# Graph attention layer on one core: eight unread products between two turnings, magnitudes of heads 8 to 15 a head earlier, their store made contiguous

## The chip, the cores and the metric

The kernel runs on one core of one Trainium2 chip. The metric is the device time of one launch in microseconds. A core has a matrix engine (TensorE, PE in the profile, with its weight loads shown apart as PEld), VectorE (DVE), ScalarE (ACT), GpSimd (POOL), and SyncE (SP), which here only issues DMAs. Each engine works through its own instructions in order; semaphores are the only thing that ties them together.

## The reference, cut to what matters

```python
# x: (2048, 512), adj: (2048, 2048) of zeros and ones; N = 2048, H = 16 heads, DH = 32, ALPHA = 0.2
seq = (x @ W_seq).reshape(N, H, DH)
score1 = jnp.einsum('nhd,d->hn', seq, a1)
score2 = jnp.einsum('nhd,d->hn', seq, a2)
scores = leaky_relu(score1[:, :, None] + score2[:, None, :], ALPHA)
scores = scores + (1.0 - adj)[None, :, :] * MASK_VAL
attn = softmax(scores, axis=-1)
hidden = einsum('hij,jhd->ihd', attn, seq).reshape(N, D_IN)
hidden = elu(hidden @ W_out + b_out)
return layernorm(x + hidden)
```

## The kernel before

A score is a sum of a row term and a column term, so the leaky exponential splits into two products of a row factor and a column factor, one for positive and one for negative sums. What is left of the softmax for one head is a mask (is the sum positive, and is there an edge) times a matrix of values. All masks are one byte per element and are read as fp8. The values are split into a high and a low half in f16, in `Vp`.

**Stages.** Up to about 85 us: load x, W and the adjacency matrix; PE turns x (L387) and two of the four parts of W (`turn_w`, L424), multiplies the turned W by the attention vectors (L431), and projects x (L400, then L416 for heads 8 to 15); ACT casts 16 adjacency tiles to bytes (L592), DVE patches them (L782), and SP's DMAs turn them (L316). `warm(n)` (L379) issues n products of 256 columns whose result nobody reads. From there to 450 us: the heads. Behind that: the output product (L568), elu and layer norm.

**A head.** For head h and each of 16 tiles jt, the sign of the score is made by ACT (L614) or by DVE (L811, six tiles of a head in heads 1 to 12: 2, 3, 6, 7, 12, 13); DVE then joins tiles in pairs with the edges (L816), which counts `t_ready` up by two. PE runs 16 products for each tile (L475) as soon as its pair is ready. Behind tile 7 and behind tile 15 it runs two blocks of products against the whole adjacency matrix (`adj_products`, L489, 32 products a block). The first such block of a group of four heads waits until all four heads' values are split: block 16, in the middle of head 4, waits for the values of head 7. The ring `tring` holds 16 tiles, one head's worth, so makers of the signs can be at most a head ahead of PE. When PE is through with a head, ACT copies the low sums (L652), DVE adds the high ones (`join`, L879, behind tile 4 of the next head), and PE may begin the next head.

**Values.** Beside head h (1 to 12) DVE and ACT make the values of head h + 3: DVE's product (L860, behind tile 1), ACT's high halves (L631), DVE's low halves (`split_low`, L866, behind tile 9). Values are scaled by a power of two taken from the largest magnitude of the head. For heads 8 to 15 this is found in three steps. DVE takes the largest of four parts (`largest`, L792) at the places in the table `MAX_AT`, and joins them in head 3 behind tile 14 (L979, `mx2_ready`). SP stores the 128 x 8 maxima to DRAM (L349, `maxima`) and loads them back spread over all partitions (L351, 128 x 1024), before it loads the row of head 5 (L352). SP gets there only once all pairs of head 3 are joined. DVE takes the largest of each head (L982, in head 4 behind tile 7), makes the powers, and goes on. L982 stands ahead of the pair of tiles 8 and 9 and of the low halves of head 7.

The order on every engine is written out by hand; no scheduler changes it. `DVE_TILES`, `MAX_AT`, `HIGH_AT` and `LOW_AT` say behind which tile something stands.

Of the kernel before, what the change touches and what calls it, by code (L numbers as in the profile page):

```python
# [10 lines left out]
ALU = mybir.AluOpType  # L11
ACT = mybir.ActivationFunctionType
AX = mybir.AxisListType

P = 128
# [49 lines left out]

FIRST_AT, ROUND_AT = {9: (0, 1), 15: (2,)}, {15: (0, 1)}

MAX_AT = {(2, 9): 0, (2, 13): 1, (3, 5): 2, (3, 9): 3}

SUMS_AT = (None,) + (4,) * (H - 1)  # L70
VALUES_AT, HIGH_AT, LOW_AT = 1, 6, 9
# [22 lines left out]
def gat_kernel(nc, x, adj, W_seq, a1, a2, W_out, b_out, out):  # L94
    with ExitStack() as ctx:
# [3 lines left out]
        def sem(name):  # L99
            return ctx.enter_context(nc.semaphore(name))  # L100
# [27 lines left out]
        peaks = flat[:, 10 * HV:10 * HV + 2 * P * HALF].bitcast(F32)  # L128
# [3 lines left out]
        ones, mx, mx2, mcol = misc[:, 0:P], misc[:, 128:128 + MC], misc[:, 160:160 + HALF], misc[:, 192:193]  # L132
# [22 lines left out]
        def pair(k):  # L155
# [19 lines left out]
        scratch2 = nc.dram_tensor("maxima", [1, P * HALF], F32, kind="Internal")  # L175
# [17 lines left out]
        mx2_part, mx2_ready, mx2_stored, peaks_loaded, peak_made = (  # L193
            sem(s) for s in ("mx2_part", "mx2_ready", "mx2_stored", "peaks_loaded", "peak_made"))
# [78 lines left out]
        def row(h):  # L273

            return abc[:, (h + 1) % 2, :] if h > 0 else row0
# [18 lines left out]
        def _(sp):  # L294
# [46 lines left out]
            for h in range(1, H):  # L341
                if h == 2:
                    sp.wait_ge(seq2_made, NT)
                if h >= 2:
                    sp.wait_ge(t_ready, NT * (h - 1))
                if h == 5:

                    sp.wait_ge(mx2_ready, 1)
                    sp.dma_start(scratch2.rearrange("o (h p) -> (o p) h", p=P), mx2, allow_slow_non_contiguous=True).then_inc(mx2_stored, 16)  # L349
                    sp.wait_ge(mx2_stored, 16)  # L350
                    sp.dma_start(peaks, scratch2[0:1, :].partition_broadcast(P)).then_inc(peaks_loaded, 16)  # L351
                sp.dma_start(row(h), scratch[h:h + 1, :].partition_broadcast(P)).then_inc(abc_loaded[h % 2], 16)  # L352
# [22 lines left out]
        def _(pe):  # L375
            def warm(n, into=bank[2]):

                for _ in range(n):
                    pe.matmul(into[:, 0:2 * P], ones16[:, 0:P], ones16, start=True, stop=True)  # L379
# [39 lines left out]
            def turn_w(n):  # L419

                k = BY_PE[n]
                pe.wait_ge(w_loaded[k], 16)
                for j in range(KT):
                    mm = pe.transpose(bank[6 + n][:, j * P:(j + 1) * P], Wx[:, k, j // 2, j % 2 * P:(j % 2 + 1) * P], idf)  # L424
                mm.then_inc(w_turned, 1)
# [26 lines left out]
            pe.wait_ge(ident, 1)  # L452
            turn_x(0)
            turn_w(0)
            turn_w(1)
            warm(4)
            pe.wait_ge(block_ready, 1)
# [92 lines left out]
            for i in range(NT + 1):  # L550
# [7 lines left out]
                if i >= 1:  # L558
                    q = (i - 1) % 2
# [197 lines left out]
        def _(dve):  # L757
# [208 lines left out]
            for h in range(1, H):  # L966
                row_loaded(dve, h)
                for jt in range(NT):
                    if jt + 1 in DVE_TILES[h]:
                        compare(h, jt + 1)  # L970
                    if jt % 2 == 1:
                        made(h, jt // 2)
                        join_adj(jt // 2, WHOLE).then_inc(t_ready, 2)
                    if (h, jt) in MAX_AT:
                        dve.wait_ge(seq2_copied, NT)
                        largest(MAX_AT[h, jt], mxd[:, MAX_AT[h, jt], :], slice(HALF, H)).then_inc(mx2_part, 1)
                    if h == 3 and jt == 14:
                        dve.wait_ge(mx2_part, 4)
                        dve.tensor_reduce(mx2, mxd.rearrange("p c k -> p k c"), AX.X, ALU.max).then_inc(mx2_ready, 1)  # L979
                    if h == 4 and jt == 7:  # L980
                        dve.wait_ge(peaks_loaded, 16)
                        dve.tensor_reduce(mx2, peaks.rearrange("p (h q) -> p h q", q=P), AX.X, ALU.max).then_inc(peak_made, 1)  # L982
                        dve.wait_ge(peak_made, 1)
                        powers(slice(HALF, H), mx2, 1)
                    if h == 4 and jt == 10:
# [186 lines left out]
```

## Time and profile before

| | us |
|---|---|
| median of 3 runs | 518.84 (518.45 to 519.27) |
| the profiled execution | 522.9 |
| its span | 521.2 |
| PE busy | 503.4 (97%) |
| DVE busy | 459.6 (88%) |
| ACT busy | 433.7 (83%) |
| L475, mask products, 4096 | 241.8 |
| L489, adjacency products, 2048 | 127.7 |

The span is the time between the first and the last instruction that the profiler saw; 1.7 us of the profiled execution lie around it. Its time is 4.1 us above the median of the three runs without a profiler. A busy share is an average over the whole span: what matters in a stretch is which engine the others wait for there, and that is read from the chain of waits and from the timelines.

### The profile page before, as it was taken

The numbers are of one execution on the slowest core, as the hardware profiler recorded it, in microseconds if no ns is written. First come the engines' busy times: TensorE is split into PE (matmuls) and PEld (weight loads), VectorE is DVE, ScalarE is ACT, GpSimd is POOL, SyncE is SP. The second block draws the span as 40 slices with busy tenths as digits, with TensorE's granted clock in tenths as the row PEclk, the third lists the DMA queues.
The fourth block names the chain that finished last, engine by engine and source line by source line (L and its number), as shares of the span: only waits on it lengthen the run. The fifth ranks groups of instructions, "written<-read, shape, count | busy, mean of one in ns | idle before, by whom it ended". The sixth has DMA issues, their size and how long they took to land.

```text
span 521.2 us, 15251 instructions
## 1 busy us (share of the span) xinstructions
PE 503.4 (97%) x6744; PEld 456.7 (88%) x6744; DVE 459.6 (88%) x577; ACT 433.7 (83%) x462; POOL 34.8 (7%) x64
## 2 busy tenths in 40 slices
PE   7999999999999989999999999999999999899993
PEld 5788889999999889999999999999999999644542
DVE  3266899998999898999999999999998879988886
ACT  2477899798999887999999999999995989356664
POOL 3000000000000010000000000000000000035444
PEclk9899999999999989999999999999999999999998
DMA  7999995202020411201021120202202040015343
GB/s 258 395 302 344 333 332 142 86 3 82 3 83 2 115 38 55 83 3 82 3 83 31 54 83 3 83 1 83 79 7 82 3 143 3 1 62 159 122 141 122
DMA packets 31617, 53.28 MB, mean 102 GB/s; under 512 B 19392, under 2 KB 20672, under 8 KB 27584
## 3 DMA queue, kind: packets, MB, share of 16 engines
q1 hardware_dynamic: 31000, 51.79, 30.5%
q8 instruction: 53, 0.87, 0.7%
q10 hardware_dynamic: 552, 0.52, 0.3%
q14 instruction: 12, 0.10, 0.1%
HBM read 43.78 MB, written 4.33 MB: 92 GB/s over the span
## 4 chain that ended last, share of the span: by engine, by line
PE 80%; DVE 9%; DMA 4%; ACT 3%; issue 2%; POOL 0%; ACTq 0%; POOLq 0%; DVEq 0%
PE sums L475 35%; PE bank L489 19%; PE sums L568 10%; PE sums L400 6%; PE sums L416 4%; DVE tring L816 3%; ACT tring L614 2%; DVE tring L811 2%; DMA maxima<-Vp 2%; PE sums L387 1%; PE bank L416 1%; PE bank L556 1%; DMA Vp<-in_L_gnn_W_seq_dram 1%; DMA Vp<-maxima 1%; DVE Vp L792 1%
## 5 line engine op out<-in xcount | busy, mean ns | idle before, releaser
L614 ACT ACTIVATE tring<-abc,ab 128x2048 int8<-128x2048 f32 x150 | 292.2, 2019 | 2.0 <-PE sums L475 2.0
L475 PE MATMUL sums<-Vp,tring 128*128 128x132 f16 x4096 | 241.8, 221 | 3.5 <-issue 2.4
L475 PEld LDWEIGHTS sums<-Vp,tring 128*128 128x128 fp8e4 x4096 | 236.9, 98 | 5.5 <-issue 3.5
L816 DVE TENSOR_TENSOR tring<-adj,tring 128x1024 uint32<-128x1024 uint32 (+1 forms) x134 | 155.9, 1174 | 13.6 <-ACT tring L614 9.1
L489 PE MATMUL bank<-Vp,adj 128*128 128x132 f16 x2048 | 127.7, 222 | 2.1 <-DVE Vp L866 2.1
L489 PEld LDWEIGHTS bank<-Vp,adj 128*128 128x128 fp8e4 x2048 | 123.8, 97 | 2.3 <-DVE Vp L866 2.3
L811 DVE TENSOR_SCALAR tring<-abc,ab 128x2048 int8<-128x2048 f32 x90 | 115.5, 1283 | 0.0
L568 PE MATMUL sums<-abc,Vp 128*128 128x512 f32 (+1 forms) x136 | 57.5, 568 | 0.1
L568 PEld LDWEIGHTS sums<-abc,Vp 128*128 128x128 f32 x136 | 24.7, 190 | 22.7 <-issue 22.0
L652 ACT ACTIVATE low<-sums 128x33 f32<-128x33 f32 (+3 forms) x66 | 20.1, 393 | 24.1 <-PE sums L475 24.0
L592 ACT ACTIVATE tring<-Vp 128x2048 int8<-128x2048 f32 x16 | 30.6, 1911 | 1.2 <-DMA Vp<-in_adj_dram 1.2
L752 ACT ACTIVATE Vp<-Vp 128x512 f32<-128x512 f32 x15 | 12.2, 813 | 16.4 <-POOL Vp L1145 16.4
L879 DVE TENSOR_TENSOR cab<-low,sums 128x66 f32<-128x66 f32 (+3 forms) x33 | 21.2, 682 | 1.9 <-ACT low L652 1.9
L637 ACT ACTIVATE acc<-bank 128x132 f32<-128x132 f32 x64 | 18.6, 290 | 4.1 <-PE bank L489 3.3
L866 DVE SCALAR_TENSOR_TENSOR Vp<-Vp,xp 128x528 f16<-128x528 f16 x32 | 21.2, 706 | 0.1
L860 DVE TENSOR_TENSOR xp<-acc,Es 128x1056 f32<-128x1056 f32 x16 | 20.0, 1252 | 0.1
L631 ACT ACTIVATE Vp<-xp 128x528 f16<-128x528 f32 x32 | 19.6, 677 | 0.6 <-DVE xp L860 0.6
L400 PE MATMUL sums<-Vp,acc 128*128 128x288 f32 x64 | 19.0, 441 | 0.0
L787 DVE COPY ab<-sums 128x32 f32<-128x32 f32 x16 | 3.0, 189 | 17.0 <-PE sums L400 17.0
L743 ACT ACTIVATE Vp<-Vp 128x512 f32<-128x512 f32 (+1 forms) x17 | 10.2, 602 | 8.3 <-DVE Vp L1041 8.2
L1041 DVE TENSOR_TENSOR Vp<-sums,Vp 128x512 f32<-128x512 f32 (+1 forms) x17 | 11.2, 658 | 6.6 <-PE sums L568 6.6
L811 DVE TENSOR_SCALAR tring<-cab,ab 128x2048 int8<-128x2048 f32 (+2 forms) x16 | 14.7, 951 | 2.3 <-ACT cab L601 2.2
(116 smaller groups left out, 369.7 us busy)
## 6 DMA issues: line engine op xcount, KB each, us to landing
Vp<-in_adj_dram SPq DMA_DIRECT2D x16, 1024.0 KB, 8.1
abc<-a_rows SPq DMA_DIRECT2D x15, 1024.0 KB, 4.8
abc<-in_x_dram SPq DMA_DIRECT2D x16, 256.0 KB, 7.4
Vp<-in_x_dram SPq DMA_DIRECT2D x16, 256.0 KB, 2.9
out_dram<-Vp SPq DMA_DIRECT2D x16, 256.0 KB, 2.0
abc<-in_L_gnn_W_out_dram SPq DMA_DIRECT2D x1, 1024.0 KB, 5.3
Vp<-in_L_gnn_W_seq_dram ACTq DMA_DIRECT2D x2, 256.0 KB, 5.4
Vp<-in_L_gnn_W_seq_dram SPq DMA_DIRECT2D x2, 256.0 KB, 6.1
```

Source lines behind the costliest of these rows:

```text
L400: mm = pe.matmul(first_bank(t), xT_part(t, k), Wx[:, k, 0, :], start=(k == BY_VECTOR[0]), stop=(k == BY_VECTOR[1]))
L416: mm = pe.matmul(second_bank(t), xT_part(t, k), Wx[:, k, 1, 0:half], start=(k == 0), stop=(k == KT - 1))
L475: mm = pe.matmul(bank[b][:, c * 2 * VW:(c + 1) * 2 * VW], slot(jt)[:, it * P:(it + 1) * P].bitcast(F8), Vp[:, h, jt, :, :], start=(jt == 0 ...
L489: mm = pe.matmul(bank[6 + s % 2][:, 0:GRP * HW], edge_bytes[:, jt // 2, it * P:(it + 1) * P, jt % 2].bitcast(F8), Vp[:, GRP * g:GRP * (g + ...
L568: mm = pe.matmul(into, hT[:, q, k * P:(k + 1) * P], Wo_sb[:, k, c], start=(k == 0), stop=(k == KT - 1))
L592: act.activation(tring[:, it, :], stage[:, it % STAGE, :], ACT.Copy, scale=EDGE, accum_out=deg[:, r:r + 1]).then_inc(adj_cast, 1)
L614: return act.activation(slot(jt)[:, columns], row(h)[:, columns], ACT.Sign, bias=ab[:, jt, H + h:H + h + 1], scale=-1.0)
L652: copied = act.activation(into, made, ACT.Copy, scale=1.0 / LO[s])
L811: return dve.tensor_scalar(slot(jt)[:, columns], row(h)[:, columns], ab[:, jt, H + h:H + h + 1], -1.0, ALU.is_gt, ALU.mult)
L816: return dve.tensor_tensor(words, edges, words, ALU.bitwise_and)
L866: low = dve.scalar_tensor_tensor(out=Vp[:, k, :, 1, s * HW:(s + 1) * HW], in0=Vp[:, k, :, 0, s * HW:(s + 1) * HW], scalar=-LO[s], in1=xp[: ...
L879: return dve.tensor_tensor(into, lo, high, ALU.add)
```

## The change

Four edits. In PE's code, eight unread products stand between the turning of W's part 1 and that of part 3. In the table `MAX_AT`, the four partial magnitudes move from heads 2, 2, 3, 3 to heads 1, 1, 2, 2; what joins them stays in head 3 behind tile 14. The store of the maxima writes the eight values of a partition side by side (32 bytes) instead of 512 bytes apart. The reduction of what is loaded back (L982, L983 in the changed kernel) reads accordingly: the 128 values of a head are 32 bytes apart in its input, where they were side by side. The extra line in PE's code makes every later line number greater by one.

```diff
-MAX_AT = {(2, 9): 0, (2, 13): 1, (3, 5): 2, (3, 9): 3}
+MAX_AT = {(1, 9): 0, (1, 13): 1, (2, 9): 2, (2, 13): 3}
...
-                    sp.dma_start(scratch2.rearrange("o (h p) -> (o p) h", p=P), mx2, allow_slow_non_contiguous=True).then_inc(mx2_stored, 16)
+                    sp.dma_start(scratch2.rearrange("o (p h) -> (o p) h", p=P), mx2).then_inc(mx2_stored, 16)
...
             turn_w(0)
+            warm(8)
             turn_w(1)
...
-                        dve.tensor_reduce(mx2, peaks.rearrange("p (h q) -> p h q", q=P), AX.X, ALU.max).then_inc(peak_made, 1)
+                        dve.tensor_reduce(mx2, peaks.rearrange("p (q h) -> p h q", q=P), AX.X, ALU.max).then_inc(peak_made, 1)
```

On PE, near the start: x's first tile is turned (L387), then W's parts 1 and 3 (L424, `w_loaded1` and `w_loaded3`). Before:

```order
5 L379 MATMUL sums<-Vp 128x256 x5
6 L387 MATMUL sums<-Vp,abc 128x128 [waits x_loaded0,ident]
7 L387 MATMUL sums<-Vp,abc 128x128 x3
8 L424 MATMUL bank<-Vp 128x128 [waits w_loaded1]
9 L424 MATMUL bank<-Vp 128x128 x3
10 L424 MATMUL bank<-Vp 128x128 [waits w_loaded3]
11 L424 MATMUL bank<-Vp 128x128 x3
12 L379 MATMUL sums<-Vp 128x256 x4
```

The same place in the changed kernel:

```order
8 L424 MATMUL bank<-Vp 128x128 [waits w_loaded1]
9 L424 MATMUL bank<-Vp 128x128 x3
10 L379 MATMUL sums<-Vp 128x256 x8
11 L424 MATMUL bank<-Vp 128x128 [waits w_loaded3]
12 L424 MATMUL bank<-Vp 128x128 x3
13 L379 MATMUL sums<-Vp 128x256 x4
```

The eight products stand ahead of the wait for W's part 3, in the place where PE had nothing to do.

On DVE, in head 3 from its join of head 2's sums (L879) to the low halves (L866) and the last pair. Before:

```order
174 L879 TENSOR_TENSOR cab<-low,sums 128x990 [waits low_copied]
175 L879 TENSOR_TENSOR cab<-low,sums 128x66
176 L811 TENSOR_SCALAR tring<-abc,ab 128x2048 [waits t_free]
177 L816 TENSOR_TENSOR tring<-adj,tring 128x1024 [waits u_ready]
178 L792 TENSOR_REDUCE Vp<-acc 128x8 [waits seq2_copied]
179 L811 TENSOR_SCALAR tring<-abc,ab 128x2048 [waits t_free]
180 L816 TENSOR_TENSOR tring<-adj,tring 128x1024 [waits above]
181 L816 TENSOR_TENSOR tring<-adj,tring 128x1024 [waits u_ready]
182 L792 TENSOR_REDUCE Vp<-acc 128x8 [waits seq2_copied]
183 L866 SCALAR_TENSOR_TENSOR Vp<-Vp,xp 128x16x33 [waits high_made]
```

And in the changed kernel:

```order
176 L880 TENSOR_TENSOR cab<-low,sums 128x990 [waits low_copied]
177 L880 TENSOR_TENSOR cab<-low,sums 128x66
178 L812 TENSOR_SCALAR tring<-abc,ab 128x2048 [waits t_free]
179 L817 TENSOR_TENSOR tring<-adj,tring 128x1024 [waits u_ready]
180 L812 TENSOR_SCALAR tring<-abc,ab 128x2048 [waits t_free]
181 L817 TENSOR_TENSOR tring<-adj,tring 128x1024 [waits above]
182 L817 TENSOR_TENSOR tring<-adj,tring 128x1024 [waits u_ready]
183 L867 SCALAR_TENSOR_TENSOR Vp<-Vp,xp 128x16x33 [waits high_made]
```

Two reductions are gone from between the pairs of head 3. They now stand in head 1, one ahead of the low halves of head 4 and one behind the pair of tiles 12 and 13 (the last rows are the first pair of head 2):

```order
139 L817 TENSOR_TENSOR tring<-adj,tring 128x1024 [waits above]
140 L817 TENSOR_TENSOR tring<-adj,tring 128x1024 [waits u_ready]
141 L793 TENSOR_REDUCE Vp<-acc 128x8 [waits seq2_copied]
142 L867 SCALAR_TENSOR_TENSOR Vp<-Vp,xp 128x16x33 [waits high_made]
...
147 L817 TENSOR_TENSOR tring<-adj,tring 128x1024 [waits above]
148 L793 TENSOR_REDUCE Vp<-acc 128x8 [waits seq2_copied]
149 L817 TENSOR_TENSOR tring<-adj,tring 128x1024 [waits u_ready]
150 L812 TENSOR_SCALAR tring<-abc,ab 128x2048 [waits t_free,abc_loaded0]
151 L817 TENSOR_TENSOR tring<-adj,tring 128x1024 [waits u_ready]
```

SP's order does not change.

## Rows read from the trace of the kernel before

**Rows 1.** The page's chain that ended last, shares of the span by engine.

```profile
PE 80%; DVE 9%; DMA 4%; ACT 3%; issue 2%; POOL 0%; ACTq 0%; POOLq 0%; DVEq 0%
```

**Rows 2.** The same chain in order of time: start us, us, what.

```profile
90.34 11.98 PE sums L475 x208
...
166.78 8.62 DMA maxima<-Vp
175.41 5.54 DMA Vp<-maxima
...
185.20 5.54 PE bank L489 x64
190.74 7.37 PE sums L475 x128
198.10 3.79 PE bank L489 x64
```

**Rows 3.** PE's timeline: start us, us, engine line what xcount [idle before <-releaser].

```profile
157.19 0.23 PE L475 MATMUL sums<-Vp,tring 128*128 128x132 f16 x1 [0.26 <-DVE tring L816]
...
175.38 7.70 PE L475 MATMUL sums<-Vp,tring 128*128 128x132 f16 x127 [1.04 <-issue]
```

**Rows 4.** DVE's timeline, from the end of head 3 to the join in head 5.

```profile
165.54 1.21 DVE L816 TENSOR_TENSOR tring<-adj,tring 128x1024 uint32<-128x1024 uint32 x1
...
167.87 1.22 DVE L816 TENSOR_TENSOR tring<-adj,tring 128x1024 uint32<-128x1024 uint32 x1
...
180.98 1.22 DVE L982 TENSOR_REDUCE Vp<-Vp 128x8 f32<-128x1024 f32 x1 [2.10 <-DMA Vp<-maxima]
...
199.47 1.19 DVE L879 TENSOR_TENSOR cab<-low,sums 128x990 f32<-128x990 f32 x1 [0.24 <-ACT low L652]
```

**Rows 5.** Landing times of the four stores of 32 KB at L337.

```profile
DMA to landing us min/median/max: 2.0/2.0/2.2
```

**Rows 6.** ACT's timeline around the store of the maxima.

```profile
164.86 2.02 ACT L614 ACTIVATE tring<-abc,ab 128x2048 int8<-128x2048 f32 x1
...
175.93 0.28 ACT L637 ACTIVATE acc<-bank 128x132 f32<-128x132 f32 x1 [0.80 <-remote]
```

**Rows 7.** DMA queues from 166.8 to 175.4 us: packets, MB, share of 16 engines.

```profile
q1 hardware_dynamic: 1040, 0.00, 5.4%
q14 instruction: 1, 0.01, 2.2%
```

**Rows 8.** Stretches: us, busy us (x) of PE, PEld, DVE, ACT, POOL; PEclk, DMA share, GB/s.

```profile
11.10:17.50 6.40, 6.40 (x24) 5.10 (x24) 1.77 (x3) 0.92 (x3) 0.00 (x0) 0.51 1.02 422
185.20:188.20 3.00, 3.00 (x28) 3.00 (x29) 3.00 (x5) 3.00 (x3) 0.00 (x0) 0.51 0.00 0
200.00:300.00 100.00, 99.58 (x1712) 99.27 (x1710) 97.52 (x98) 97.66 (x89) 0.00 (x0) 1.00 0.12 44
```

**Rows 9.** DVE's timeline in heads 2 and 3.

```profile
121.21 1.23 DVE L816 TENSOR_TENSOR tring<-adj,tring 128x1024 uint32<-128x1024 uint32 x1 [1.53 <-ACT tring L614]
...
133.17 1.23 DVE L816 TENSOR_TENSOR tring<-adj,tring 128x1024 uint32<-128x1024 uint32 x1 [0.94 <-ACT tring L614]
...
153.39 1.21 DVE L792 TENSOR_REDUCE Vp<-acc 128x8 f32<-128x1024 f32 x1
```

**Rows 10.** PE's timeline at the turning of W's part 3.

```profile
9.14 0.66 PE L424 MATMUL bank<-Vp 128*128 128x128 f32 x4 [1.88 <-DMA Vp<-in_L_gnn_W_seq_dram]
9.63 0.60 PE L379 MATMUL sums<-Vp 128*128 128x256 f16 x4
```

**Rows 11.** ACT's and DVE's timelines ahead of head 0.

```profile
73.27 1.91 ACT L592 ACTIVATE tring<-Vp 128x2048 int8<-128x2048 f32 x1 [0.64 <-DMA Vp<-in_adj_dram]
...
92.02 5.97 DVE L816 TENSOR_TENSOR tring<-adj,tring 128x512 uint32<-128x512 uint32 x8
```

**Rows 12.** The two small reductions, by line: duration ns min/median/max, starts, form.

```profile
L979 DVE TENSOR_REDUCE Vp<-Vp x1: 199/199/199, 165.4 to 165.4; 128x8 f32<-128x32 f32 x1
L857 DVE TENSOR_REDUCE Vp<-Vp x1: 322/322/322, 56.5 to 56.5; 128x24 f32<-128x96 f32 x1
```

## The prediction, made before the changed kernel was run

> **What bounds the kernel now.** I read the page's chain of waits first, then the same chain in order of time, then the timelines of the engines where it leaves PE. By engine, PE holds 80% of the chain and DVE and DMA hold most of the rest [rows 1]. The reader is to see that this rest is not spread evenly. From 200 to 300 us PE works 99.6% of the time at the full clock, with DVE and ACT at 97.5 and 97.7% [rows 8]: there PE is the bound, the other two keep up with little to spare, and what PE gains ahead of that stretch stays gained. The exception is one place in head 4. The chain goes through the store of the maxima, 8.62 us for 4 KB, and their load, 5.54 us, and ends in PE's block 16, which starts at 185.20 and takes 5.54 us for 64 products where its like takes 3.79 [rows 2]. DVE stood 2.10 us ahead of L982 until that load had landed [rows 4], and behind L982 in DVE's queue stand the pair of tiles 8 and 9 and the low halves of head 7, for which block 16 waits. PE had ended the first half of head 4 at 183.08 (175.38 + 7.70, [rows 3]), so it idled 2.12 us, and in the 3 us from its restart the granted clock was 0.51, the lower of its two levels, 1.2 instead of 2.4 GHz [rows 8]. So the one late load costs PE 2.12 us of idling and 5.54 - 3.79 = 1.75 us of slow products.
>
> The start has a slow stretch too: from 11.1 to 17.5 us the clock was 0.51 [rows 8], after PE had idled 1.88 us ahead of W's part 3 [rows 10].
>
> **The change part by part.**
>
> *The store.* It had 1040 packets for 1024 values, so each value went by itself [rows 7]. The changed one has one run of 32 bytes for each partition. The nearest rows are the stores of 32 KB at L337, 2.0 to 2.2 us to landing [rows 5]; its other bound is no gain at all, 8.62. I take 2.2: those stores also go to DRAM in runs of many values, which is what the edit makes of this one. Saved: 6.4 us of the load's start.
>
> *The magnitudes.* Each costs 1.21 us on DVE [rows 9]. Two of them leave head 3, so its last pair, joined by 166.75 (165.54 + 1.21, [rows 4]), can be joined up to 2.4 us earlier, at 164.4. SP waits for just that pair before the store (issue at 166.78, [rows 2]). So the store goes out at 164.4, lands by 166.6, and the load lands 5.54 us later, by 172.1 instead of 180.95.
>
> *What they cost in heads 1 and 2.* Two reductions come into head 1, 2.4 us. Behind it DVE idles for ACT twice, 1.53 us at the first pair of head 2 and 0.94 us later in head 2 [rows 9], 2.47 us in all, and ACT's signs there do not depend on DVE. So the delay is used up by 133 us. Queued behind the two are the last pairs of head 1 and the join of head 1's sums. PE does not reach those pairs before its second half of head 1, and the join, 0.9 us later than now, still ends about when PE ends its blocks. I count nothing. If that cover is gone it costs PE at most 0.9 us there.
>
> *DVE in head 4.* It does not keep the 2.4 us. The first pair of head 4 needs a sign that ACT ends at 166.88 (164.86 + 2.02, [rows 6]), where DVE began that pair at 167.87 [rows 4]. DVE is then 1.0 us earlier and held by ACT. It comes to the reduction of the loaded maxima at 178.88 - 1.0 = 177.9 (180.98 less its idle 2.10, [rows 4]) and finds them landed since 172.1. It starts 3.1 us earlier than now.
>
> *The reduction L983.* Its input is now read 32 bytes apart. It took 1.22 us [rows 4]. The one row that reads with the same step is L979, 32 values in 199 ns; L857, with a wider step, took 322 ns for 96 [rows 12]. By their difference, 123 ns for 64 values or 1.9 ns a value, 1024 values take 2.1 us with L979's start; if L979's whole time were reading, at 6.2 ns a value, they take 6.4. At the 1.2 ns a value of L982 as a whole, L979's 32 values are 38 ns and the other 161 a fixed start; that reading needs no cost of the step. So I take 1.22, keep 2.1 for the range, and make a rival of 6.4. The Trainium skill speaks against this edit (SBUF — State Buffer, in Door 1: The DMA port swizzle): SBUF has lines of 16 bytes, and each access that crosses to a new line pays a penalty; with 32 bytes between values every read would. It gives no figure; by that rule the sum would lean to the 2.1 us and lose 0.9.
>
> *PE in head 4.* It gains 0.26 us in head 3, where it waited for a pair that stands behind the first removed reduction. It stood 1.04 us at the start of head 4 for nothing that the profile shows, until 175.38, and ACT 0.80 us until 175.93 [rows 3, 6]. The store landed at 175.4. In its time an instruction fetch took 3.0 us (2.2% of 16 engines times 8.6 us, [rows 7]). I read both stalls as instructions held up behind the single-value writes, and let them go with those. So PE ends the first half of head 4 at 183.08 - 0.26 - 1.04 = 181.8, and what is late next is the low halves of head 7, 3.1 us earlier than now, at 182.1. Block 16 starts there instead of at 185.20. An idle of 0.3 us is shorter than the 1.04 us that left the clock up, so the 64 products take 3.79 us: 3.1 + 1.75 = 4.85 us earlier behind them.
>
> *Head 5.* Who is late next is DVE's join of head 4's sums. It ended at 200.66 (199.47 + 1.19, its wait for ACT being 0.24, [rows 4]). It moves by 3.1 + 0.24, to 197.3. PE would be through with its blocks at 201.89 - 4.85 = 197.0 (198.10 + 3.79, [rows 2]). It waits 0.3 us, and 4.5 us are left. From there on all engines work in step.
>
> *The eight products at the start.* Four of their kind took 0.60 us [rows 10], so eight end within 1.2 us, inside the 1.88 us of idling: no cost, and an idle of 0.7 us or more remains. If the clock then stays up, the 6.4 us at 0.51 shrink by up to 3.2. But this lead meets two fixed points. ACT's cast at 73.27 waited for the adjacency matrix to arrive [rows 11], which PE does not speed up. And DVE joins the rest of head 0's pairs from 92.02, the first by 92.6 [rows 11], while PE comes for it at 93.1 (90.34 and 48 of 208 products in 11.98 us, [rows 2]). So PE has 0.5 us of slack and must wait out the rest of its lead, up to 2.7 us. An idle of 1.88 and one of 2.12 us stood ahead of the two low stretches above, so this one may bring another, at 1.75 us. Bounds: a gain of 1.0 (the slack and as much again from small waits of ACT and DVE), a loss of 1.2 (0.5 less 1.75). I count 0, as the edit changes nothing on the path that sets head 0's pairs.
>
> **Sum.** 4.5 us. The profiled execution was 522.9 (a span of 521.2 and 1.7 around it) and would be 518.4. Taken from the median of 518.84 it is **514.3**. The profiled run is 4.1 above the median, and I cannot see which of its waits the other runs lack; that is in the range.
>
> **The rivals.**
>
> *The start pays as well.* For it: PE is held by nothing else there. Against: the two fixed points. 1.0 more: 513.3.
>
> *The clock falls in head 4 all the same, or did not fall in the runs without a profiler.* For it: 0.3 us of idling is a difference of times each known to some tenths, and L983 at 2.1 us makes it 1.2. Then 1.75 us of the sum go, 516.1, and with L983's 0.9 us, 517.0.
>
> *The lead at the start is paid back.* PE waits for head 0's pairs long enough for the clock to fall: 1.2 us lost, 515.5.
>
> *The store does not do what it should.* If the 8.62 us are the way to DRAM and back and not the packets, only the magnitudes act: the load lands at 164.4 + 8.6 + 5.54 = 178.6, DVE waits 0.7 us, the two stalls stay, and block 16 starts at 182.8. That is 2.4 + 1.75 us, less 0.3 at the join: 514.9. For it: the writes' own packets took only 5.4% of the stretch [rows 7].
>
> *Slower than before: the reading of L983.* At 6.4 us it ends 5.2 us later than I have it. Block 16 starts at 187.3, 2.1 us later than now, at the low clock as now: 520.9. It decides from 4.3 us on (1.22 + 3.1); beyond it the edit that saves the store costs more than the wait. Against it: no reduction in this trace is that slow per value unless its start is counted in.
>
> **How the numbers follow.** Forecast 0.50, start pays 0.12, clock 0.15, start pays back 0.12, slow store 0.06, slow reading 0.05. The point is the forecast's, 514.3. The range takes in the first three whole and most of the next: 512.5 to 517.0; what is left out is the slow reading, and the ends of the others where two of them meet. A measurement of this kernel tells about 0.2%, 1 us, from no change. Faster 0.90; no change 0.05, where the clock and the start go wrong together; slower 0.05.
>
> **What would show it.** In the trace after: the store lands about 2 us from its issue, and this issue is near 164.4; L983 has no idle ahead of it and takes 1.2 us; PE's stall at the start of head 4 and ACT's are gone; block 16 starts near 182 and takes 3.8 us; the clock shows no low stretch there. The join ahead of head 5 ends near 197.3 with a short wait of PE. At the start, the clock stays at 1.00 from 11 to 17.5 us, PE's products of head 0's rest nonetheless start near 93, and the idle is ahead of them. I am wrong if L983 is over 2 us, if DVE is late at the join of head 1, or if a low clock stands at another place.

## The result, and the profile after

The changed kernel takes 516.54 us (median of 6 runs, 516.36 to 516.71). The kernel before, run beside it, takes 519.27 (median of 5 runs, 518.45 to 520.60; a sixth took 1828.31 us and is left out, with it the median would be 519.88). The ratio is 0.9948 with a 95% interval of 0.9933 to 0.9964: 0.5% or 2.7 us faster, where 4.5 us were forecast. The time lies inside the range, the sign is right, and the size is 60% of what I had worked out.

The profiled execution of the changed kernel took 516.55, with a span of 514.8. Its page (busy us, share of the span, instructions; then the chain that ended last by engine and by line):

```profile
PE 501.1 (97%) x6752; PEld 455.5 (88%) x6752; DVE 460.1 (89%) x577; ACT 433.7 (84%) x462; POOL 34.9 (7%) x64
...
PE 86%; ACT 6%; DVE 5%; issue 2%; POOL 0%; POOLq 0%; DVEq 0%; ACTq 0%
```

No DMA is left in the chain, where it had 4% [rows 1]. The chain through head 4 now runs over ACT and DVE alone (start us, us, what):

```profile
162.29 1.90 ACT tring L615
...
164.29 1.23 DVE tring L817
...
174.08 1.22 DVE tring L817
175.30 1.95 DVE Vp L983
...
178.77 1.42 DVE Vp L867 x2
180.19 0.05 issue
180.24 3.96 PE bank L490 x64
```

SP's DMAs (start us, us of issuing), and from the view of the DMAs from 161.8 to 170 us the queue of instruction fetches (packets, MB, share of 16 engines) and the time from issue to landing:

```profile
161.81 0.32 SPq L349 DMA_DIRECT2D maxima<-Vp  x1
163.21 0.32 SPq L351 DMA_DIRECT2D Vp<-maxima  x1
```

```profile
q14 instruction: 1, 0.01, 0.2%
...
Vp<-maxima SPq DMA_DIRECT2D x1, 512.0 KB, 4.5
maxima<-Vp SPq DMA_DIRECT2D x1, 4.0 KB, 1.4
```

The store lands in 1.4 us instead of 8.62 [rows 2], and the load by 167.7 (163.21 + 4.5). DVE comes for it only at 175.22, so 7.5 us of slack are left. DVE's timeline (start us, us, what, and in brackets the idle time ahead and what ended it):

```profile
160.57 1.21 DVE L817 TENSOR_TENSOR tring<-adj,tring 128x1024 uint32<-128x1024 uint32 x1
161.70 1.28 DVE L812 TENSOR_SCALAR tring<-abc,ab 128x2048 int8<-128x2048 f32 x1
164.29 1.23 DVE L817 TENSOR_TENSOR tring<-adj,tring 128x1024 uint32<-128x1024 uint32 x1 [1.31 <-ACT tring L615]
...
175.22 2.02 DVE L983 TENSOR_REDUCE Vp<-Vp 128x8 f32<-128x1024 f32 x1
```

The idle ahead of the reduction [rows 4] is gone, and DVE waits for ACT's sign at head 4's first pair, as foreseen. But the reduction takes 2.02 us instead of 1.22. PE's timeline from head 4 to head 5:

```profile
170.85 7.53 PE L476 MATMUL sums<-Vp,tring 128*128 128x132 f16 x128
180.24 3.96 PE L490 MATMUL bank<-Vp,adj 128*128 128x132 f16 x64 [1.86 <-DVE Vp L867]
184.04 7.53 PE L476 MATMUL sums<-Vp,tring 128*128 128x132 f16 x128
191.41 3.95 PE L490 MATMUL bank<-Vp,adj 128*128 128x132 f16 x64
195.60 7.53 PE L476 MATMUL sums<-Vp,tring 128*128 128x132 f16 x128 [0.24 <-issue]
```

The stall of 1.04 us at head 4's start [rows 3] is gone. PE still idles 1.86 us ahead of block 16, where 0.3 was forecast, and yet the 64 products behind it ran at the full clock: 3.96 us instead of 5.54.

Against the trace of before all this would be a gain of 6.4 us of span. That is more than the 2.7 us of the medians, because the traced execution of before was one with the low clock in two places, and most executions have a higher mean clock than that one. The granted clock of each execution sorts the times. Of the 14 traces of this document, the four with a mean of 0.993 or less have a low stretch between the first full clock and the last 6 us of the span, and the ten with 0.994 or more have none there. (Time ahead of the first full clock is not counted as low: the trace with the full clock only from 19.4 us has 0.996.) Over 81 executions of the kernel before, and 24 of the changed kernel (12 with the eight unread products, 12 without, which take the same time, as shown below):

| mean granted clock of the execution | executions of before | median us | executions of the changed kernel | median us |
|---|---|---|---|---|
| 0.994 or more | 22 | 518.54 | 19 | 516.50 |
| 0.991 to 0.993 | 56 | 519.92 | 3 | 516.97 |
| 0.990 or less | 3 | 521.75 to 522.65 | 2 | 518.42 and 518.97 |

The trace that I predicted from had 0.986 and 522.9. Two things are read from the table. Among executions with the clock up, the change is worth 2.0 us (518.54 to 516.50). And it makes a low clock rarer: 59 of 81 executions have 0.993 or less before, 5 of 24 after. The other 0.7 us between the medians fit that (an estimate: the share falls by 0.52, and the first two groups of before lie 1.38 us apart).

### The profile page after: what moved, and what is told of

Its sections match the earlier page's. It is cut to its first block, busy times and chain, and to the rows that moved or that the text cites. A ratio compares the mean times of both kernels' runs of the same rounds, so it can differ in the third digit from the quotient of the medians.

```text
span 514.8 us, 15267 instructions
## 1 busy us (share of the span) xinstructions
PE 501.1 (97%) x6752; PEld 455.5 (88%) x6752; DVE 460.1 (89%) x577; ACT 433.7 (84%) x462; POOL 34.9 (7%) x64
## 4 chain that ended last, share of the span: by engine, by line
PE 86%; ACT 6%; DVE 5%; issue 2%; POOL 0%; POOLq 0%; DVEq 0%; ACTq 0%
PE sums L476 39%; PE bank L490 20%; PE sums L569 10%; PE sums L400 6%; ACT tring L615 5%; PE sums L416 4%; DVE tring L817 1%; PE sums L387 1%; PE bank L416 1%; PE bank L557 1%; PE sums L379 1%; DVE tring L812 1%; DVE acc L893 0%; DVE acc L889 0%; DVE Vp L983 0%
## 5 line engine op out<-in xcount | busy, mean ns | idle before, releaser
L490 PE MATMUL bank<-Vp,adj 128*128 128x132 f16 x2048 | 126.1, 221 | 1.9 <-DVE Vp L867 1.9
L490 PEld LDWEIGHTS bank<-Vp,adj 128*128 128x128 fp8e4 x2048 | 122.2, 96 | 2.1 <-DVE Vp L867 2.0
L1042 DVE TENSOR_TENSOR Vp<-sums,Vp 128x512 f32<-128x512 f32 (+1 forms) x17 | 11.2, 658 | 6.6 <-PE sums L569 6.6
L400 PE MATMUL sums<-Vp,acc 128*128 128x288 f32 x64 | 17.0, 406 | 0.0
```

What stands on the lines that cost most here:

```text
L400: mm = pe.matmul(first_bank(t), xT_part(t, k), Wx[:, k, 0, :], start=(k == BY_VECTOR[0]), stop=(k == BY_VECTOR[1]))
L490: mm = pe.matmul(bank[6 + s % 2][:, 0:GRP * HW], edge_bytes[:, jt // 2, it * P:(it + 1) * P, jt % 2].bitcast(F8), Vp[:, GRP * g:GRP * (g + ...
```

## The experiments

**The kernel before once more**, to have a trace of it without the low clock.

> The kernel before itself, to see how its runs spread. Theory C (clock): its executions differ in whether TensorE's clock has its low stretch at the start (worth about 2.7 us) and in head 4 (1.75 us). Times then lie in groups near 518.5, 520.2 to 520.9 and 522.9, and the shorter the time, the higher the mean granted clock. Rival P (even): the spread is noise of the measurement, one group near 519.5, and mean clock says nothing about the time.

Measured: 520.0 (12 runs), ratio 1.0002 (0.9988 to 1.0016). Its profiled execution took 519.23 with a mean clock of 0.995 and no low stretch at the start or in head 4. PE's timeline there:

```profile
171.57 0.22 PE L475 MATMUL sums<-Vp,tring 128*128 128x132 f16 x1
172.82 7.71 PE L475 MATMUL sums<-Vp,tring 128*128 128x132 f16 x127 [1.03 <-issue]
182.93 3.96 PE L489 MATMUL bank<-Vp,adj 128*128 128x132 f16 x64 [2.41 <-DVE Vp L866]
...
198.29 6.90 PE L475 MATMUL sums<-Vp,tring 128*128 128x132 f16 x117 [0.25 <-issue]
```

Granted clock (the 1.00 behind POOL's columns) from 11.1 to 17.5 us, and from 183 to 187 us, where block 16 ran:

```profile
11.10:17.50 6.40, 6.40 (x41) 5.38 (x41) 1.36 (x5) 3.01 (x5) 0.00 (x0) 1.00 1.02 417
...
183.00:187.00 4.00, 4.00 (x69) 4.00 (x70) 4.00 (x6) 4.00 (x4) 0.00 (x0) 1.00 0.01 4
```

So the same kernel idles 2.41 us there and keeps its clock, where the first trace idled 2.12 us and lost it. A stall of about 1.03 us and an idle of 2.1 to 2.4 us are in both traces; the low clock is not. This trace, and not the first, is the one to hold against the trace after when the steps of the code are compared. Head 5 begins at 198.29 in the one and at 195.60 in the other: 2.69 us. It is not the typical execution of before: only 2 of these 12 have 0.994 or more, the other ten have 0.992 or 0.993 and a median of 520.1, and even among the 22 of the table it stands 0.7 us above the median. What the others gain on it is not recorded.

**The magnitudes alone, and the store alone.**

```diff
-MAX_AT = {(2, 9): 0, (2, 13): 1, (3, 5): 2, (3, 9): 3}
+MAX_AT = {(1, 9): 0, (1, 13): 1, (2, 9): 2, (2, 13): 3}
```

> Only the magnitudes a head earlier; store and read as before. The store goes out 2.4 us earlier relative to head 0 and lands 8.6 us later, the load 5.8 later. If PE's stall of 1.03 and ACT's of 0.88 us at head 4 come from the single-value store, they stay, 2.4 us earlier or in another place. DVE waits for the load 1 us (now 2.38), with the reduction at 1.22 us, so block 16 starts 2.1 us earlier than in a run of before without low stretches (182.93): 180.8 to 181, and the time is 1.5 to 2 us under the kernel before. If the magnitudes were not what holds the store, nothing moves.

```diff
-  sp.dma_start(scratch2.rearrange("o (h p) -> (o p) h", p=P), mx2, allow_slow_non_contiguous=True)
+  sp.dma_start(scratch2.rearrange("o (p h) -> (o p) h", p=P), mx2)
...
-  dve.tensor_reduce(mx2, peaks.rearrange("p (h q) -> p h q", q=P), AX.X, ALU.max)
+  dve.tensor_reduce(mx2, peaks.rearrange("p (q h) -> p h q", q=P), AX.X, ALU.max)
```

> Only the contiguous store and its read; magnitudes as before. The store lands 1.4 us from its issue as in the changed kernel (8.6 before), the load is there before DVE comes, and L982 takes 2.02 us instead of 1.22. DVE's wait of 2.38 us goes and 0.8 us come back: block 16 starts 1.6 us earlier, and head 5 by as much: 1.6 us under the kernel before, about 517.7. If the stalls of PE and ACT at head 4 come from the single-value store, both are gone here and stay in the run with the magnitudes alone. If they come from the load that follows, they are here too.

Measured: the magnitudes alone 517.69 (10 runs), ratio 0.9959 (0.9943 to 0.9976); the store with its reading alone 517.26 (10 runs), ratio 0.9964 (0.9946 to 0.9982). Each gives most of the gain by itself, and they don't add up (the two intervals overlap, so the runs don't order them). DVE's timeline of the magnitudes alone shows what is left without the store:

```profile
176.57 1.22 DVE L982 TENSOR_REDUCE Vp<-Vp 128x8 f32<-128x1024 f32 x1 [0.99 <-DMA Vp<-maxima]
```

Counted from the start of head 0's rest, so that differences of the load phase fall out, block 16 begins after 92.53 us in the kernel before, 90.26 with the magnitudes alone (2.27 earlier), 90.86 with the store alone (1.67 earlier), and 90.01 with both (2.52 earlier). Both remove the same wait for the load. In the magnitudes' trace the 64 products of block 16 took 5.54 us, behind an idle of 2.13; in the store's they took 3.96, behind one of 2.17. Part of the magnitudes' loss is the clock: 3 of their 10 executions have 0.994 or more, and these took 516.4 (median), no more than the changed kernel's; the six of the store alone took 517.0. In the traces the magnitudes' block 16 begins 0.25 us behind the changed kernel's (90.26 and 90.01). With the clock up, then, the contiguous store and its strided reading add little to the magnitudes, on the evidence of three executions. Both lines are of PE's timeline:

```profile
180.79 5.54 PE L489 MATMUL bank<-Vp,adj 128*128 128x132 f16 x64 [2.13 <-DVE Vp L866]
```

```profile
180.61 3.96 PE L489 MATMUL bank<-Vp,adj 128*128 128x132 f16 x64 [2.17 <-DVE Vp L866]
```

The magnitudes' trace also settles what the single-value store holds up. Its instruction fetch, from 161.8 to 170.9 us, took 2.3% of 16 engines, 3.3 us (in the trace after 0.2% of 16 engines over 8.2 us, 0.3 us):

```profile
q1 hardware_dynamic: 1040, 0.00, 5.2%
q14 instruction: 1, 0.01, 2.3%
```

Yet neither PE nor ACT stalled at the start of head 4, which came after the store had ended. The stalls (PE 1.03 to 1.36 us, ACT 0.88 us in the kernel before once more) stood, besides [rows 3, 6], in the three other traces in which the store still ran as head 4 began, and in none of the ten in which it did not. That the fetch is held up by the single-value store is shown; that the stall is a fetch held up at the wrong moment fits all traces, and no run removed the fetch alone.

**The reading side by side.** The changed kernel with the reduction reading as before. It then takes each maximum over the wrong values of the eight heads.

```diff
-  dve.tensor_reduce(mx2, peaks.rearrange("p (q h) -> p h q", q=P), AX.X, ALU.max)
+  dve.tensor_reduce(mx2, peaks.rearrange("p (h q) -> p h q", q=P), AX.X, ALU.max)
```

> The changed kernel, but its reduction reads values that stand side by side, so it takes the largest over the wrong groups of heads (the powers of two by which values are scaled differ, no instruction does). If 32 bytes between values are what makes it 2.02 us, it takes 1.22, block 16 starts 0.8 us earlier, and since DVE has no idle from there to the join ahead of head 5 the time falls by 0.8 us, to 515.7. If the 2.02 us are for another reason (the values just landed by DMA, a DMA beside it), it stays at 2.02 and 516.5.

Measured: 515.93 (6 runs), ratio 0.9936 (0.9919 to 0.9953). The reduction, grouped by line (ns: mean, least, most), here and in the changed kernel:

```profile
L983 DVE TENSOR_REDUCE Vp<-Vp x1: 1211/1211/1211, 177.2 to 177.2; 128x8 f32<-128x1024 f32 x1
```

```profile
L983 DVE TENSOR_REDUCE Vp<-Vp x1: 2019/2019/2019, 175.2 to 175.2; 128x8 f32<-128x1024 f32 x1
```

The same 1024 values cost 0.81 us more when 32 bytes lie between them, and head 5 begins 0.82 us later for it (105.37 against 104.55 us from head 0's rest). The Trainium skill (SBUF — State Buffer, in Door 1: The DMA port swizzle) has reads that cross to a new line pay; the trace agrees in direction, and gives the size, 0.79 ns a value.

**The low halves ahead of the reduction.** The changed kernel with the reduction, the powers and the scale factors three tiles later, so that block 16 waits for neither.

```diff
-                    if h == 4 and jt == 7:
+                    if h == 4 and jt == 10:
                         dve.wait_ge(peaks_loaded, 16)
...
-                    if h == 4 and jt == 10:
+                    if h == 4 and jt == 11:
                         scale_factors(1, slice(HALF, H))
```

> The changed kernel with the reduction L983 and the powers moved from tile 7 to tile 10 of head 4, behind the pair of tiles 8 and 9 and the low halves of head 7. If PE's wait of 1.86 us ahead of block 16 is now only DVE's 1.95 us reduction and 0.4 us of powers standing ahead of the low halves, the wait goes: block 16 starts about 1.9 us earlier, and the time is 514.7. If the wait is for something else (ACT's high halves, DVE being behind as a whole), the time stays at 516.5. DVE does the same work, so if DVE is what bounds heads 4 and 5, half or more of the gain is lost again at the join ahead of head 5: 515.7.

Measured: 517.52 (12 runs), ratio 0.9964 (0.9952 to 0.9976), 1 us slower than the changed kernel. PE's timeline, then one line of DVE's:

```profile
178.66 3.96 PE L490 MATMUL bank<-Vp,adj 128*128 128x132 f16 x64 [0.19 <-DVE Vp L867]
...
187.47 3.86 PE L476 MATMUL sums<-Vp,tring 128*128 128x132 f16 x64 [1.16 <-DVE tring L817]
...
196.53 7.53 PE L476 MATMUL sums<-Vp,tring 128*128 128x132 f16 x128 [1.41 <-issue]
```

```profile
176.14 1.23 DVE L817 TENSOR_TENSOR tring<-adj,tring 128x1024 uint32<-128x1024 uint32 x1 [0.74 <-ACT tring L615]
```

The ratio's interval overlaps that of the changed kernel, but all 12 executions took 517.21 to 517.72, and 11 of the 12 of the changed kernel took 516.72 or less. Block 16 begins 1.58 us earlier, with 0.19 us of idling, and head 5 begins 0.93 later. The idle ahead of block 16 was not PE's loss to begin with: PE gives it back as 1.16 us at a pair and 1.41 at head 5. What sets head 5 is DVE's whole row of work in head 4, and the moved reduction only uncovered 0.74 us in which DVE waits for ACT (counted from head 0's rest, head 5 begins 0.82 us later).

**The maxima in two steps.** If DVE's work is the bound, shortening it must pay in full. The changed kernel, with the 1024 maxima loaded first as 16 partitions of 64 values, reduced to 16 x 8 behind tile 2, stored, and loaded to all partitions as 128 values each:

```diff
-  sp.dma_start(peaks, scratch2[0:1, :].partition_broadcast(P)).then_inc(peaks_loaded, 16)
+  sp.dma_start(few, scratch2.rearrange("o (g x) -> (o g) x", g=16)).then_inc(few_loaded, 16)
+  sp.wait_ge(few_made, 1)
+  sp.dma_start(scratch3.rearrange("o (g h) -> (o g) h", g=16), few_max).then_inc(few_stored, 16)
+  sp.wait_ge(few_stored, 16)
+  sp.dma_start(peaks[:, 0:16 * HALF], scratch3[0:1, :].partition_broadcast(P)).then_inc(peaks_loaded, 16)
...
+                    if h == 4 and jt == 2:
+                        dve.wait_ge(few_loaded, 16)
+                        dve.tensor_reduce(few_max, few.rearrange("p (q h) -> p h q", h=HALF), AX.X, ALU.max).then_inc(few_made, 1)
```

> The changed kernel with the maxima brought in by two small loads: 16 partitions load 64 values each and reduce them (about 0.26 us, behind tile 2 of head 4), their 16 x 8 results are stored and spread to all partitions, and the last reduction reads 128 values instead of 1024 (about 0.4 us instead of 2.02). DVE's work in head 4 falls by 1.4 us. If DVE bounds the stretch from head 4 to the join ahead of head 5, block 16 and head 5 start 1.4 us earlier: 515.1. If the second trip through DRAM lands too late (it has from 168 to 175 us), DVE waits there again and the gain is gone. If PE bounds the stretch, block 16 starts earlier and head 5 does not.

Measured: 515.06 (514.93 to 515.44, 4 runs), ratio 0.9916 (0.9896 to 0.9936): 1.5 us below the changed kernel, and the fastest version here, with the reference's whole computation. DVE's timeline, then PE's:

```profile
167.77 0.25 DVE L990 TENSOR_REDUCE Vp<-Vp 16x8 f32<-16x64 f32 x1
...
175.20 0.38 DVE L993 TENSOR_REDUCE Vp<-Vp 128x8 f32<-128x128 f32 x1
```

```profile
178.64 3.96 PE L497 MATMUL bank<-Vp,adj 128*128 128x132 f16 x64 [0.28 <-DVE Vp L874]
...
194.00 7.53 PE L483 MATMUL sums<-Vp,tring 128*128 128x132 f16 x128 [0.24 <-issue]
```

DVE has 2.02 - 0.25 - 0.38 = 1.39 us less to do, and head 5 begins 1.60 us earlier. The second way through DRAM and back fits into the slack that the contiguous store left.

**The eight products.** Alone in the kernel before; the changed kernel without them, twice; the kernel above without them; and the changed kernel once more as the measure.

```diff
             turn_w(0)
+            warm(8)
             turn_w(1)
```

> Only the eight unread products. Theory C: the low stretch at the start is gone in every run, and the lead stays: 518.5 to 518.8 where head 4 keeps its clock, 520.3 where it loses it; nothing near 522.9. Rival P (my prediction's step: the lead is waited out ahead of head 0): within 0.5 us of the kernel before, and PE's products of head 0's rest start at the same 93 us as before.

> The changed kernel without the eight products. Theory C: head 4 is as in the changed kernel (block 16 waits 1.9 us, 2.3 us earlier than before relative to the heads), but the start's low stretch comes back in some or all runs: 516.5 where it does not, 519.2 where it does. Rival P: 516.5 in all runs, the eight products being worth nothing.

> The changed kernel without the eight unread products, once more: 516.3 if they are worth nothing. If they keep the clock up at the start, this one has runs near 518 to 519 with a clock near 0.990 that the changed kernel has not.

> The changed kernel once more, beside the next one on the same chip: 516.5, clock 0.994 to 0.997. If the low stretch at the start can come in it as well, some run stands 1 to 2.5 us above, with a clock near 0.990.

> The two-step maxima without the eight unread products at the start. If these products are worth nothing, 515.0 as with them; if they keep the clock up at the start in some runs, this one has runs near 517 that the other lacks.

Measured: alone 520.37 (12 runs), ratio 1.0015 (1.0001 to 1.003). The changed kernel without them 516.31 and 516.84 (6 runs each; ratios 0.9943 and 0.9944), with them 516.54 and 516.66 (0.9948 and 0.9938): over 12 runs of each kind 516.54 against 516.55. The two steps without them 515.35, with them 515.06, inside one another's intervals (0.9894 to 0.9925, 0.9896 to 0.9936). In the changed kernel they are worth nothing that can be measured. Alone in the kernel before they cost 0.15% or 0.8 us, and the interval just leaves out no change: all 12 executions had 0.992 or 0.993, where 12 of the 29 of the kernel before beside them had 0.994 or more. Why is not shown. PE's timeline of the changed kernel, and of the side-by-side kernel, which has the same start:

```profile
7.47 1.06 PE L424 MATMUL bank<-Vp 128*128 128x128 f32 x4
8.32 1.65 PE L379 MATMUL sums<-Vp 128*128 128x256 f16 x8
9.81 0.60 PE L424 MATMUL bank<-Vp 128*128 128x128 f32 x4
```

```profile
6.21 1.04 PE L379 MATMUL sums<-Vp 128*128 128x256 f16 x8
8.44 0.66 PE L424 MATMUL bank<-Vp 128*128 128x128 f32 x4 [1.19 <-DMA Vp<-in_L_gnn_W_seq_dram]
```

In the first, PE came late, the products ran at the low clock and took the place of no idle. Of 14 traces, eight have a start of this kind: the full clock comes at 9.2 to 10.5 us and no low stretch follows at the start, with the products or without. In one it comes at 19.4 us. In five it comes at 3.8 to 4.3 us. Three of these lose it again at 10.6 to 11.2 us, behind an idle ahead of W's part 3 of 1.88 us (before), 1.32 (the magnitudes alone) and 1.19 (the side-by-side kernel, which has the eight products). Two keep it, behind 0.61 us (the changed kernel again) and 0.20 us (the same without the products). The idle there depends on when W's part 3 lands, and the products don't fill it.

**Unread products in head 4.** In the kernel before, 16 of them ahead of block 16's wait, into a bank that is free there, to see whether they spare PE the low clock.

```diff
+                if s == 16:
+                    pe.wait_ge(adj_copied, 15)
+                    warm(16, into=bank[6])
                 pe.wait_ge(v_ready, GRP * (g + 1))
```

> The kernel before with 16 unread products (1.8 us) ahead of PE's wait for block 16, in the 2.1 to 2.4 us that it idles there. Nothing else changes. Theory C (what spreads the runs of before is whether the clock falls in head 4, which depends on where in its period the chip's view of PE stands when PE idles): the slow group, clock 0.992 to 0.993 and 519.0 to 520.7 us, is gone, and what is left is like the fast group: 518.4, about 1 us under the median of before. Rival: the two groups have another cause and stay; median as before.

Measured: 519.26 (12 runs), ratio 0.9999 (0.9979 to 1.0019). No gain in time. The profiled execution had a late start of its own (full clock from 19.38 us, 524.15 us in all), and in head 4:

```profile
185.48 1.91 PE L379 MATMUL bank<-Vp 128*128 128x256 f16 x16
187.88 3.96 PE L492 MATMUL bank<-Vp,adj 128*128 128x132 f16 x64 [0.48 <-DVE Vp L869]
```

The block ran at the full clock there, as it did behind 2.41 us of idling in the trace without such products. Executions at 0.992 and below still occurred, but they are rarer: 4 of 12, against 14 of 17 at 0.993 and below in the kernel before beside it. Where in them the clock was low is not recorded. So the products seem to keep the clock up more often, and yet the time is the same; those with the clock up took 518.8 (median), where the kernel before took 518.55. Whether unread products help in head 4 stays open; if they do, it is by less than the measurement tells.

## Why the prediction was right or wrong

Two terms of the sum failed. The price of the low clock in head 4 was put at 1.75 us and charged to every execution; where the clock falls there it costs about 1.4 us, it seems to fall in most executions of before and in a few of the changed kernel, and the medians hold about 0.7 us of it by my estimate. And the reduction that reads with a step was put at no cost and took 0.80 us more. The rest of the mechanism held. The second trace of before against the trace after gives the sum term by term, without the low clock, which neither has:

| step | forecast us | measured us | from |
|---|---|---|---|
| L983 starts earlier | 3.1 | 3.49 | 178.71 to 175.22 |
| L983 takes longer | 0 | -0.80 | 1.22 to 2.02 |
| the low clock goes | 1.75 | not in these two traces; about 0.7 between the medians, by the table of clocks | 3.96 and 3.96 |
| the join at head 5 | -0.3 | 0 | 0.25 and 0.24 of waiting |
| head 5 starts earlier | 4.5 | 2.69 | 198.29 to 195.60 |

The second trace of before began head 0's rest 0.17 us later (90.40 and 90.23), so 2.52 of the 2.69 us are head 4's.

**The store and the load: right, and better than put.** 1.4 us instead of my 2.2, which doesn't matter with 7.5 us of slack. That the 8.62 us were the way to DRAM and back, the slow-store rival, is refuted. So is that rival's claim that the other edit alone would keep the stalls: with the magnitudes alone they were gone too, because head 4 began after the store.

**The magnitudes: right.** They left the waits of heads 1 and 2 to use up: DVE's idle of 1.53 us is gone and that of 0.94 us is down to 0.33 in the trace after, and PE shows nothing there. DVE was held by ACT's sign at head 4 as worked out. The start of L983 moved by 3.49 us, 0.28 of the 0.39 us above the forecast because its idle in the second trace of before was 2.38 us and not 2.10:

```profile
178.71 1.22 DVE L982 TENSOR_REDUCE Vp<-Vp 128x8 f32<-128x1024 f32 x1 [2.38 <-DMA Vp<-maxima]
```

**L983: wrong, and it was the choice between ends.** I took 1.22 us, by the reading that L979's 199 ns are mostly a fixed start. The upper bound of 2.1, by the difference of L979 and L857 [rows 12], was the measured 2.02. The rule of the Trainium skill (SBUF — State Buffer, in Door 1: The DMA port swizzle) that a read crossing to a new line pays spoke for it. I set it aside because it had no figure; two rows had one. This term took 0.80 us. The slower-than-before rival, 6.4 us, is refuted.

**The clock in head 4: wrong, the largest part.** The step "an idle of 0.3 us is shorter than the 1.04 us that left the clock up" had two faults. The idle is 1.86 us. Counted from the start of head 0's rest, PE ended its first half of head 4 at 88.15 us where I had 88.9 (178.38 - 90.23, and 181.8 - 92.94), since the stall with what lay around it was worth more than 1.04 us, and block 16 began at 90.01 where I had 89.2, since the reading took 0.80 longer. And the clock does not follow from the idle: 2.41 us left it up in one execution of before, 2.1 us did not in another. The 1.75 us were counted as if every execution paid them, and they were mis-sized besides: 5.54 us is a block behind an idle, 3.79 one that follows on others, and beside its like behind an idle, 3.96 us, the low clock costs 1.58. DVE's join is then no longer waited for, so less of it reaches head 5: with the eight products alone, whose trace had the low clock, head 5 began 1.10 us later, from head 0's rest, than in the trace without it (108.99 and 107.89), and the time from head 5 to the end was 0.3 us longer (319.5 and 319.2 us). That is 1.4 us in all, and the first two groups of before lie 1.38 us apart. So my second rival, that the runs without a profiler did not have the low clock, came true in part only: 22 of 81 executions had none by their mean. Its 517.0 is near the measured 516.54, but not for its reason alone.

The low stretch in the trace with the eight products alone, granted clock 0.51 from 184.5 to 188 us:

```profile
184.50:188.00 3.50, 3.50 (x36) 3.50 (x34) 3.50 (x5) 3.50 (x4) 0.00 (x0) 0.51 0.02 5
```

PE's timeline in the same trace:

```profile
183.12 5.54 PE L490 MATMUL bank<-Vp,adj 128*128 128x132 f16 x64 [2.28 <-DVE Vp L867]
...
199.65 5.51 PE L476 MATMUL sums<-Vp,tring 128*128 128x132 f16 x93
```

Over the versions, the clock mostly stays up more often the shorter the idle ahead of block 16. The idle is from each version's trace; the last column counts the executions with a mean of 0.994 or more:

| version | idle us | clock up |
|---|---|---|
| the eight products alone | 2.28 | 0 of 12 |
| the kernel before | 2.12 and 2.41 | 22 of 81 |
| the magnitudes alone | 2.13 | 3 of 10 |
| the store alone | 2.17 | 6 of 10 |
| the changed kernel, with the products or without | 1.86 to 1.88 | 19 of 24 |
| the reading side by side | 1.05 | 4 of 6 |
| unread products in head 4 | 0.48 | 8 of 12 |
| the maxima in two steps, with the products or without | 0.28 | 7 of 10 |
| the low halves first | 0.19 | 12 of 12 |

The mean does not say where the clock was low, and a short low stretch at the start also lowers it, so this is a relation over whole executions and no threshold. The maxima in two steps without the products have three executions at 0.992 and 0.993 that took only 0.5 us more than the other three: theirs was hardly in head 4.

**PE in head 4 and the join.** The stall's end was worth nothing by itself. It ended PE's half earlier, and PE then waited longer for block 16. At head 5, DVE's join is the limit in both kernels: in the trace after it ends at 195.50, and PE starts head 5 at 195.60.

```profile
194.19 1.31 DVE L880 TENSOR_TENSOR cab<-low,sums 128x990 f32<-128x990 f32 x2
```

DVE does not idle from the pair at 164.29 until that join, so the sum is DVE's, and the two kernels that changed DVE's work there (1 us slower, 1.5 us faster) show it. The 0.3 us that I took off at the join was a wait already there, 0.25 us.

**The start: the zero was right, the reason only in part.** I called ACT's cast at 73.27 a fixed point, because it waited for the adjacency matrix. In the undisturbed trace of before and in the trace after it stands at 71.60 and 70.86, still waiting for that DMA:

```profile
71.60 1.91 ACT L592 ACTIVATE tring<-Vp 128x2048 int8<-128x2048 f32 x1 [0.87 <-DMA Vp<-in_adj_dram]
```

```profile
70.86 1.91 ACT L593 ACTIVATE tring<-Vp 128x2048 int8<-128x2048 f32 x1 [0.88 <-DMA Vp<-in_adj_dram]
```

So that transfer's landing is no fixed point. Head 0's rest began at 92.94 in the trace I predicted from, at 92.24 and 95.40 in two others with a long low or late clock at the start, and at 89.8 to 90.8 in the eleven that are left, with the eight products or without them. The 2.7 us between 92.94 and the changed kernel's 90.23 are again which execution was traced: the kernel before once more has 90.40.

**The level.** I took the difference from the median and not from the profiled run, which was right: the profiled run was 4.1 us too high. But I then let its low clock stand in the sum. The gap between the two was the hint that a part of what I saw was not in every run.

## What to carry to other kernels

When the profiled execution is slower than the median of the plain runs, look for what only it has before pricing it: a clock that fell in one execution is worth its share of the executions, before and after the change, and another profile of the same kernel costs less than a wrong term. A wait on PE ahead of a block is PE's loss only if nothing else sets the next meeting point; add up the other engine's work to that point first, and shorten that. A contiguous store that makes a later read strided moves a cost from a queue with slack onto the busiest engine; reducing in two small steps avoided both.

## What the runs showed of the hardware

A DVE reduction of 1024 f32 values in each partition took 1.21 us with the values side by side and 2.02 us with 32 bytes from one to the next.

A store of 4 KB as 1024 single values took 8.62 us to landing, as 128 runs of 32 bytes 1.4 us. During the first an instruction fetch took 3.0 to 3.3 us instead of 0.3, and where head 4 began in that time PE stood 1.03 to 1.36 us for nothing that the profile shows.

The granted clock is not a function of the program alone. In the same kernel, an idle of about 2.1 to 2.4 us ahead of the same block left the clock up in one trace and took it to 0.51 in another, 1.2 instead of 2.4 GHz. The full clock was first granted at 3.8 to 4.3 us, at 9.2 to 10.5 us, or at 19.4 us of the span. Over the versions, a shorter idle there mostly went with the clock up in more executions, for instance 22 of 81 where PE idled 2.1 to 2.4 us ahead of the block, 19 of 24 where it idled 1.9.
